# Four sixteen-head attention stages: the exponential of a step split by head and bank

## Chip, cores and metric

The kernel runs on one core of a Trainium2 chip. The metric is device time in microseconds (us) of one execution; lower is better. The core has TensorE (PE), VectorE (DVE), ScalarE (ACT), GpSimd (POOL) and SyncE (SP, which only starts DMAs). Each takes its own instructions in order, and semaphores order them among engines.

## The reference, cut to what matters

The network is a chain of 16 residual layers on X of shape 8 x 512 x 128. Four of them are attentions with 16 heads of 8 channels: `l0b` (no mask), and `l2a`, `l2b`, `l3a` (causal). What such a layer computes for each batch and head is, in short:

```
q, k, v = heads(x @ Wq), heads(x @ Wk), heads(x @ Wv)   # 16 heads of 8 channels
scores  = einsum('bhqd,bhkd->bhqk', q, k)               # 512 x 512, * 1/sqrt(8) and causal in l2a, l2b, l3a
attn    = softmax(scores, axis=-1)
out     = einsum('bhqk,bhkd->bhqd', attn, v)            # l2a, l2b, l3a: then a projection
```

The other twelve layers (experts, quantised feed-forward, other attentions) are not touched.

## The kernel before

All four attentions are built by `heads_attention_stage` (L475). Its work is cut into steps T. A step takes one pair of heads (hh = 0, 1) and one chunk c of the key tiles. A group of four heads (index g, four per batch) has L steps (index l): L = 8 in l0b, where a chunk is one tile of 128 keys against all 512 queries, and L = 6 in the causal stages, where the chunks are key tile 0 (512 query columns), key tile 1 (384) and key tiles 2 and 3 together (256 + 128 columns). With 8 batches, l0b has 256 steps and each causal stage 192.

Every engine walks the same loop over T, written out by hand:

- **TensorE**, step T: `scoresT(T)` (L707) makes the transposed scores of the step in `ps_t`, which has two PSUM banks, one per head. The two matmuls of a key tile, one per head, use different halves of the array's rows and run side by side. On even T follow `scores` (L733) for the steps T+3L and T+3L+1, the untransposed scores from which the maxima of the softmax are taken, in two buffers `ps_s`. On odd T follows `values` (L756), the product of the exponentials of the steps T-3 and T-2 with v. Then come the odd jobs of `spare` (L783), which share the one bank `ps_x`: projections q, k, v (g = 0, 1), the transposes "max", "back" (l = 3 in every group), "attnT", and the output projection.
- **ScalarE**, step T: at l = 2 first `read_group` (L839), a copy of the finished group's values (`oT`); then `exponentials(T)` (L830), one operation over both heads' banks, 1024 columns or 768, from `ps_t` to the SBUF tile `E`.
- **VectorE**, step T: `maxima` (L988) of step T+3L, the divisions, the splitting of the maxima, and in l0b the copies `l0b_y` (L1057).
- **GpSimd**, causal stages: `keep` (L905) zeroes the masked part of the exponentials.

`ps_t` is one buffer. So `scoresT(T)` waits until the exponential of step T-1 has ended, and the exponential of T waits for the matmuls of T; the wait of TensorE stands at the head of its queue, with `scores` or `values` of the step behind it. Only in the last steps (T from LAST = ALL - 3L + 2), when `scores` are all done, the two buffers `ps_s` join, and the transposed scores go round three buffers.

Of the kernel before, what the change touches and what calls it, by code (L numbers as in the profile page):

```python
# [474 lines left out]
def heads_attention_stage(core, name, w, wo=None, bo=None, qk_bias=None, v_bias=None, rope=None, eps=0.0,  # L475
# [10 lines left out]
    L = 2 * NC  # L486
# [9 lines left out]
    with ExitStack() as ctx:  # L496
# [147 lines left out]
        def _(sp):  # L644
# [11 lines left out]
            def place_stack(n, half):  # L656

                for a in range(2):
                    sp.wait_ge(pieces_stored[a].sem, pieces_stored[a].after(PLACES * (n + 1)))
                if n >= 2:  # L660
                    sp.wait_ge(scoresT_ready.sem, scoresT_ready.upto((n - 2) * STEPS + (2 * half + 2) * L))
                for a, dst in enumerate((qs[n % 2], ks[n % 2])):
                    for hh in range(2):
                        sp.dma_start(dst[64 * hh:64 * hh + STACK, 4 * half:4 * half + 4, :],
                                     stack[a, :, 2 * hh + half].rearrange("k d c s -> k d (c s)")).then_inc(stack_ready[half].sem, 16)
# [42 lines left out]
        def _(pe):  # L708
            def scoresT(T, b, g, l):
# [3 lines left out]
                if T <= LAST:  # L713
                    pe.wait_ge(probs_ready.sem, probs_ready.upto(T))
                elif T <= LAST + 2:
                    pe.wait_ge(scores_read.sem, scores_read.upto(ALL))
                else:
                    pe.wait_ge(probs_ready.sem, probs_ready.upto(T - 2))
                if l == 0 and g % 2 == 0:
                    pe.wait_ge(max_placed[g // 2].sem, max_placed[g // 2].after(2 * (b + 1)))  # L720
                    if b == 0 and g == 0:
                        pe.wait_ge(ones_placed.sem, ones_placed.after(4))
                off = 0
                for kt in k_chunks[c]:
                    n = S - first_q[kt]
                    for hh in range(2):
                        r = slice(64 * hh, 64 * hh + M_ROW + 3)
                        mm = pe.matmul(scores_room(T)[:, hh, off:off + n], ks[b % 2][r, j, kt * P:(kt + 1) * P],  # L728
                                       qs[b % 2][r, j, first_q[kt]:S], start=True, stop=True)
                    off += n  # L730
                mm.then_inc(scoresT_ready.sem, 1)
# [24 lines left out]
            def values(n):  # L756
# [3 lines left out]
                pe.wait_ge(probs_ready.sem, probs_ready.upto(2 * n + 2))  # L760
# [68 lines left out]
        def _(act):  # L829
            def exponentials(T, b, g, l):  # L830
                c, p = l // 2, l % 2
                n = T // 2
                act.wait_ge(scoresT_ready.sem, scoresT_ready.upto(T + 1))
                if n >= 3:
                    act.wait_ge(pv_ready.sem, pv_ready.upto(n - 2))
                act.activation(probs(n % 3, c, 0)[:, 2 * p:2 * p + 2, :], scores_room(T)[:, :, 0:width[c]],  # L836
                               ACT.Exp, scale=scale).then_inc(probs_ready.sem, 1)
# [60 lines left out]
        def _(pool):  # L898
# [6 lines left out]
            def keep(T, b, g, l):  # L905

                c, p = l // 2, l % 2
                pool.wait_ge(probs_ready.sem, probs_ready.upto(T + 1))
# [231 lines left out]
    scores_ready.per = scores_read.per = scoresT_ready.per = probs_ready.per = ALL  # L1140
# [2589 lines left out]
```

## Time and profile before

| | us |
|---|---|
| median of 3 runs | 3916.51 |
| the runs | 3915.03, 3926.91, 3916.51 |
| the profiled execution | 3924.91 |
| its span, first to last instruction | 3923.1 |
| steps of l0b in it, 528.9 to 945.3 | 416.4 |
| steps of l2a, 1956.8 to 2280.0 | 323.2 |
| steps of l2b, 2503.8 to 2830.5 | 326.7 |
| steps of l3a, 3066.9 to 3388.2 | 321.3 |

Over the whole span the page gives TensorE busy 72%, VectorE 67%, ScalarE 45%, GpSimd 44%. The program is a chain of 16 layers, so these shares say little for one layer; the stretches in the lower half of the table are read one by one. A row of a timeline gives the start, the duration, the engine and line, and in brackets how long the engine stood idle before and what ended it. PE is the matmul, PEld the weight load ahead of it; the wait of a matmul sits on its weight load, and since matmuls are pipelined, a matmul's row ends after the array is already free for the next. An operation of ScalarE can start before the row of the one before it ends.

### The profile page before, as it was taken

How to read it: one execution, taken by the hardware profiler on the slowest of the kernel's cores; microseconds unless marked ns; L12 is line 12 of the kernel's file. 1: busy time of each engine (PE TensorE's matmuls, PEld its weight loads, DVE VectorE, ACT ScalarE, POOL GpSimd, SP SyncE). 2: the span in 40 equal slices, each digit the busy share in tenths (PEclk: the TensorE clock that was granted, in tenths of full speed). 3: DMA queues.
4: the chain of work that ended last, by engine and by line, in shares of the span. 5: the costliest groups of instructions: out<-in, count | busy, mean ns of one | idle time of the engine just before them, and what ended most of it. 6: DMA issues, size and time to landing. Idle time of an engine off the chain costs nothing. (4 is left out here: it accounts for less than half of the span.)

```text
span 3923.1 us, 64375 instructions
## 1 busy us (share of the span) xinstructions
PE 2817.3 (72%) x22261; PEld 1768.3 (45%) x22261; DVE 2638.8 (67%) x5824; ACT 1783.6 (45%) x3184; POOL 1713.8 (44%) x2364
## 2 busy tenths in 40 slices
PE   6869267775693769569488856688656888677946
PEld 4769212221693449459233335233344333354535
DVE  5645478886455944344588858688677788595768
ACT  2423247665221324334256643566643466544633
POOL 7655422220546022232456443355543555445743
PEclk9979679998797759879699977799977899886977
DMA  6123232210231012002222100222000222000000
GB/s 191 45 72 103 56 96 78 87 61 30 79 93 45 0 64 70 16 23 70 71 75 75 59 1 2 90 74 75 26 0 24 84 82 76 2 1 1 1 3 19
DMA packets 220979, 208.00 MB, mean 53 GB/s; under 512 B 49671, under 2 KB 197831, under 8 KB 219896
## 3 DMA queue, kind: packets, MB, share of 16 engines
q1 hardware_dynamic: 208376, 178.69, 14.1%
q0 software_dynamic: 12288, 25.19, 2.1%
q8 instruction: 188, 3.08, 0.3%
q14 instruction: 127, 1.04, 0.1%
HBM read 103.94 MB, written 97.91 MB: 51 GB/s over the span
## 5 line engine op out<-in xcount | busy, mean ns | idle before, releaser
L993 DVE TENSOR_REDUCE l0b_negm<-l0b_ps_s 128x2 f32<-128x1024 f32 x256 | 304.1, 1219 | 51.5 <-PE l0b_ps_s L746 50.5
L836 ACT ACTIVATE l0b_E<-l0b_ps_t 128x1024 f32<-128x1024 f32 x242 | 247.8, 1024 | 117.6 <-PE l0b_ps_t L728 117.4
L993 DVE TENSOR_REDUCE l2b_negm<-l2b_ps_s 128x2 f32<-128x256 f32 (+3 forms) x256 | 196.3, 818 | 28.7 <-PE l2b_ps_s L751 28.6
L836 ACT ACTIVATE l2a_E<-l2a_ps_t 128x768 f32<-128x768 f32 (+1 forms) x182 | 160.4, 881 | 119.7 <-PE l2a_ps_t L728 118.9
L836 ACT ACTIVATE l3a_E<-l3a_ps_t 128x768 f32<-128x768 f32 (+1 forms) x182 | 160.4, 881 | 117.1 <-PE l3a_ps_t L728 116.3
L993 DVE TENSOR_REDUCE l3a_negm<-l3a_ps_s 128x2 f32<-128x256 f32 (+3 forms) x256 | 196.3, 818 | 16.6 <-PE l3a_ps_s L751 16.5
L993 DVE TENSOR_REDUCE l2a_negm<-l2a_ps_s 128x2 f32<-128x256 f32 (+3 forms) x256 | 195.9, 816 | 14.9 <-PE l2a_ps_s L751 14.8
L836 ACT ACTIVATE l2b_E<-l2b_ps_t 128x768 f32<-128x768 f32 (+1 forms) x182 | 160.3, 881 | 100.3 <-PE l2b_ps_t L728 99.5
L913 POOL TENSOR_SCALAR_AFFINE_SELECT l2b_E<-l2b_E 128x256 f32<-128x256 f32 x256 | 100.6, 409 | 175.9 <-ACT l2b_E L836 175.7
L913 POOL TENSOR_SCALAR_AFFINE_SELECT l2a_E<-l2a_E 128x256 f32<-128x256 f32 x256 | 101.3, 408 | 161.3 <-ACT l2a_E L836 159.2
L913 POOL TENSOR_SCALAR_AFFINE_SELECT l3a_E<-l3a_E 128x256 f32<-128x256 f32 x256 | 101.3, 409 | 159.7 <-ACT l3a_E L836 157.9
L728 PE MATMUL l0b_ps_t<-room_up,room_down 51*128 51x512 bf16 x484 | 96.2, 394 | 70.2 <-ACT l0b_E L836 60.9
L775 PE MATMUL l0b_ps_v<-l0b_E,l0b_v 128*32 128x512 f32 x1024 | 140.6, 621 | 3.7 <-ACT l0b_E L836 2.1
L2934 ACT ACTIVATE l0fb_hT<-l0fb_ps_u 128x512 f32<-128x512 f32 x85 | 50.8, 598 | 145.8 <-PE l0fb_ps_u L2872 144.3
L2934 ACT ACTIVATE l0fa_hT<-l0fa_ps_u 128x512 f32<-128x512 f32 x85 | 50.8, 598 | 144.7 <-PE l0fa_ps_u L2872 143.6
L728 PEld LDWEIGHTS l0b_ps_t<-room_up,room_down 51*128 51x128 bf16 x484 | 23.3, 93 | 204.5 <-ACT l0b_E L836 193.8
L746 PE MATMUL l0b_ps_s<-room_down,room_up 48*128 48x512 bf16 x512 | 87.8, 404 | 25.7 <-DVE l0b_negm L993 22.7
L2872 PE MATMUL l0fb_ps_u<-l0fb_xT,l0fb_own_up 128*128 128x128 f32 x680 | 94.3, 284 | 10.1 <-DVE l0fb_xT L3120 4.6
L2872 PE MATMUL l0fa_ps_u<-l0fa_xT,l0fa_own_up 128*128 128x128 f32 x680 | 94.1, 283 | 9.3 <-DVE l0fa_xT L3120 4.8
L775 PE MATMUL l2b_ps_v<-l2b_E,l2b_v 128*32 128x512 f32 (+3 forms) x1024 | 93.9, 463 | 8.9 <-POOL l2b_E L913 6.9
L775 PE MATMUL l2a_ps_v<-l2a_E,l2a_v 128*32 128x512 f32 (+3 forms) x1024 | 91.7, 453 | 4.9 <-ACT l2a_oT L844 2.3
L775 PE MATMUL l3a_ps_v<-l3a_E,l3a_v 128*32 128x512 f32 (+3 forms) x1024 | 91.6, 452 | 4.7 <-ACT l3a_oT L844 2.9
(982 smaller groups left out, 8703.0 us busy)
## 6 DMA issues: line engine op xcount, KB each, us to landing
room_up<-l0b_stack SPq DMA_DIRECT2D x32, 192.0 KB
room_down<-l0b_stack SPq DMA_DIRECT2D x32, 192.0 KB
room_up<-l2a_stack SPq DMA_DIRECT2D x32, 192.0 KB
room_down<-l2a_stack SPq DMA_DIRECT2D x32, 192.0 KB
room_up<-l2b_stack SPq DMA_DIRECT2D x32, 192.0 KB
room_down<-l2b_stack SPq DMA_DIRECT2D x32, 192.0 KB
room_up<-l3a_stack SPq DMA_DIRECT2D x32, 192.0 KB
room_down<-l3a_stack SPq DMA_DIRECT2D x32, 192.0 KB
```

The lines of the kernel that those rows point to most:

```text
L728: mm = pe.matmul(scores_room(T)[:, hh, off:off + n], ks[b % 2][r, j, kt * P:(kt + 1) * P], qs[b % 2][r, j, first_q[kt]:S], start=True, sto ...
L746: mm = pe.matmul(ps[:, hh, off:off + keys[qt]], qs[b % 2][r, j, qt * P:(qt + 1) * P], ks[b % 2][r, j, 0:keys[qt]], start=True, stop=not ca ...
L775: mm = pe.matmul(ps_v[32 * a:32 * a + 32, first_q[kt]:S], v_row[b % 2][:, kt, col:col + 32], e[:, a, off:off + w_k], start=(kt == 0), stop ...
L836: act.activation(probs(n % 3, c, 0)[:, 2 * p:2 * p + 2, :], scores_room(T)[:, :, 0:width[c]], ACT.Exp, scale=scale).then_inc(probs_ready.s ...
L913: kept = pool.affine_select(out=here, in_=here, compare_op=ALU.is_ge, fill=0.0, base=0, pattern=[[0, 2], [1, P]], channel_multiplier=-1)
L993: e = dve.tensor_reduce(negm[:, qt, :, j], ps_s[n % 2][:, :, off:off + keys[qt]], AX.X, ALU.max, negate=True)
L2872: mm = pe.matmul(ps_u[j % 4][:, c, :], own_up[j % 3][:, c * P:(c + 1) * P], xT[G % 2][:, k, :], start=True, stop=True)
L2934: a = act.activation(hT[j % 3][:, :, :], ps_u[j % 4][:, :, :], ACT.Gelu)
```

## The change

Each step's exponential becomes two operations, one per head and bank, each half as long in columns (512, or 384). Each of the two waits for its own head's matmul and adds one to `probs_ready`; a step thus counts two. `scoresT` adds one to `scoresT_ready` at the last matmul of each head, and the first matmul of head hh waits for the exponential of head hh of the step before. The other waits on the two semaphores have their counts doubled, so they wait for both heads as before.

```diff
@@ scoresT @@
-                if T <= LAST:
-                    pe.wait_ge(probs_ready.sem, probs_ready.upto(T))
-                elif T <= LAST + 2:
+                if LAST < T <= LAST + 2:
                     pe.wait_ge(scores_read.sem, scores_read.upto(ALL))
-                else:
-                    pe.wait_ge(probs_ready.sem, probs_ready.upto(T - 2))
...
+                before = T if T <= LAST else T - 2
                 off = 0
                 for kt in k_chunks[c]:
                     n = S - first_q[kt]
                     for hh in range(2):
+                        if kt == k_chunks[c][0] and before > 0 and not LAST < T <= LAST + 2:
+                            pe.wait_ge(probs_ready.sem, probs_ready.upto(2 * before - 1 + hh))
                         r = slice(64 * hh, 64 * hh + M_ROW + 3)
                         mm = pe.matmul(scores_room(T)[:, hh, off:off + n], ks[b % 2][r, j, kt * P:(kt + 1) * P],
                                        qs[b % 2][r, j, first_q[kt]:S], start=True, stop=True)
+                        if kt == k_chunks[c][-1]:
+                            mm.then_inc(scoresT_ready.sem, 1)
                     off += n
-                mm.then_inc(scoresT_ready.sem, 1)
@@ exponentials @@
-                act.wait_ge(scoresT_ready.sem, scoresT_ready.upto(T + 1))
                 if n >= 3:
                     act.wait_ge(pv_ready.sem, pv_ready.upto(n - 2))
-                act.activation(probs(n % 3, c, 0)[:, 2 * p:2 * p + 2, :], scores_room(T)[:, :, 0:width[c]],
-                               ACT.Exp, scale=scale).then_inc(probs_ready.sem, 1)
+                for hh in range(2):
+                    act.wait_ge(scoresT_ready.sem, scoresT_ready.upto(2 * T + 1 + hh))
+                    act.activation(probs(n % 3, c, 0)[:, 2 * p + hh, :], scores_room(T)[:, hh, 0:width[c]],
+                                   ACT.Exp, scale=scale).then_inc(probs_ready.sem, 1)
@@ place_stack, values, keep, end of the stage: the counts doubled @@
-                pe.wait_ge(probs_ready.sem, probs_ready.upto(2 * n + 2))
+                pe.wait_ge(probs_ready.sem, probs_ready.upto(2 * (2 * n + 2)))
...
-                pool.wait_ge(probs_ready.sem, probs_ready.upto(T + 1))
+                pool.wait_ge(probs_ready.sem, probs_ready.upto(2 * (T + 1)))
```

The order of the other work stays. On ScalarE in l0b, around the copy `oT` at l = 2 of a group, there stood before (each row one operation, or several with the same waits):

```order
L836 ACTIVATE l0b_E<-l0b_ps_t 128x1024 [waits pv_ready,scoresT_ready] x8
L844 ACTIVATE l0b_oT<-l0b_ps_v 128x512 [waits spare_ready,pv_ready]
L836 ACTIVATE l0b_E<-l0b_ps_t 128x1024 [waits pv_ready,scoresT_ready]
L883 ACTIVATE l0b_mT<-l0b_ps_x 24x512 [waits max_placed1,spare_ready]
L836 ACTIVATE l0b_E<-l0b_ps_t 128x1024 [waits pv_ready,scoresT_ready] x6
```

and with the change, a pair of rows for each step:

```order
L837 ACTIVATE l0b_E<-l0b_ps_t 128x512 [waits scoresT_ready,pv_ready]
L837 ACTIVATE l0b_E<-l0b_ps_t 128x512 [waits scoresT_ready]
L845 ACTIVATE l0b_oT<-l0b_ps_v 128x512 [waits spare_ready,pv_ready]
L837 ACTIVATE l0b_E<-l0b_ps_t 128x512 [waits scoresT_ready,pv_ready]
L837 ACTIVATE l0b_E<-l0b_ps_t 128x512 [waits scoresT_ready]
L884 ACTIVATE l0b_mT<-l0b_ps_x 24x512 [waits max_placed1,spare_ready]
```

The copy `oT` (l = 2) and the odd copies still stand between the exponentials of two steps, ahead of both heads.

On TensorE in l2a, around the third chunk (256 + 128 columns, l = 4 and 5), there stands with the change:

```order
L727 MATMUL l2a_ps_t<-room_up,room_down 128x384 [waits probs_ready] x2
L775 MATMUL l2a_ps_v<-l2a_E,l2a_v_1 32x512 [waits pv_read,probs_kept,probs_ready]
L775 MATMUL l2a_ps_v<-l2a_E,l2a_v_1 32x512 x3
L801 MATMUL l2a_ps_x<-identf,l2a_oT 128x128 [waits pv_read,spare_read]
L801 MATMUL l2a_ps_x<-identf,l2a_oT 128x128 x3
L727 MATMUL l2a_ps_t<-room_up,room_down 128x256 [waits probs_ready] x2
L727 MATMUL l2a_ps_t<-room_up,room_down 128x128 x2
L746 MATMUL l2a_ps_s<-room_down,room_up 128x256 [waits scores_read]
```

where before the pairs of `l2a_ps_t` read like this, one wait for both heads:

```order
L728 MATMUL l2a_ps_t<-room_up,room_down 128x384 [waits probs_ready]
L728 MATMUL l2a_ps_t<-room_up,room_down 128x384
L775 MATMUL l2a_ps_v<-l2a_E,l2a_v_1 32x512 [waits pv_read,probs_kept,probs_ready]
L775 MATMUL l2a_ps_v<-l2a_E,l2a_v_1 32x512 x3
L801 MATMUL l2a_ps_x<-identf,l2a_oT 128x128 [waits pv_read,spare_read]
L801 MATMUL l2a_ps_x<-identf,l2a_oT 128x128 x3
```

Now both matmuls of the first key tile wait, each for its own head, and the 128-column matmul of head 0 stands behind the one of head 1 that waits.

## Rows read from the trace of the kernel before

**Rows 1.** Stretches: us; PE, PEld, DVE, ACT, POOL busy; PEclk; DMA share; GB/s.
```profile
528.90:945.30 416.40, 327.66 (x2260) 88.10 (x2260) 339.48 (x483) 291.89 (x321) 92.55 (x179) 0.97 0.21 65
1956.80:2280.00 323.20, 269.19 (x2819) 118.32 (x2814) 254.44 (x500) 201.59 (x269) 176.44 (x339) 0.97 0.18 66
```

**Rows 2.** Groups of instructions, forms apart, 528 to 944 us.
```profile
L993 DVE TENSOR_REDUCE l0b_negm<-l0b_ps_s 128x2 f32<-128x1024 f32 x234 | 279.1, 1220 | 37.3 <-PE l0b_ps_s L746 36.3
L836 ACT ACTIVATE l0b_E<-l0b_ps_t 128x1024 f32<-128x1024 f32 x241 | 246.8, 1024 | 117.6 <-PE l0b_ps_t L728 117.4
```

**Rows 3.** The same view, 1956 to 2279 us.
```profile
L836 ACT ACTIVATE l2a_E<-l2a_ps_t 128x768 f32<-128x768 f32 x121 | 98.1, 811 | 84.3 <-PE l2a_ps_t L728 84.1
```

**Rows 4.** Waits, 528 to 944 us (last columns: us in total, times, longest).
```profile
PEld l0b_ps_t L728 <- ACT l0b_E L836: 193.8, 185, 1.7
...
DVE l0b_negm L993 <- PE l0b_ps_s L746: 36.3, 50, 3.1
```

**Rows 5.** Waits, 1956 to 2279 us.
```profile
DVE l2a_negm L993 <- PE l2a_ps_s L751: 13.4, 25, 0.9
```

**Rows 6.** Timeline of l0b (start us, us, engine, line, operation, [idle before]).
```profile
669.58 0.39 PE L728 MATMUL l0b_ps_t<-room_up,room_down 51*128 51x512 bf16 x2 [0.69 <-ACT l0b_E L836]
...
670.01 1.02 ACT L836 ACTIVATE l0b_E<-l0b_ps_t 128x1024 f32<-128x1024 f32 x1 [0.49 <-PE l0b_ps_t L728]
...
671.03 0.60 ACT L844 ACTIVATE l0b_oT<-l0b_ps_v 128x512 f32<-128x512 f32 x1
...
671.53 1.02 ACT L836 ACTIVATE l0b_E<-l0b_ps_t 128x1024 f32<-128x1024 f32 x1
...
671.61 0.10 PEld L746 LDWEIGHTS l0b_ps_s<-room_down,room_up 48*128 48x128 bf16 x2 [0.41 <-DVE l0b_negm L993]
...
672.60 0.39 PE L728 MATMUL l0b_ps_t<-room_up,room_down 51*128 51x512 bf16 x2 [0.60 <-ACT l0b_E L836]
...
673.92 0.66 PE L801 MATMUL l0b_ps_x<-identf,l0b_oT 128*128 128x128 f32 x4
...
674.51 0.39 PE L728 MATMUL l0b_ps_t<-room_up,room_down 51*128 51x512 bf16 x2
...
676.02 0.39 PE L728 MATMUL l0b_ps_t<-room_up,room_down 51*128 51x512 bf16 x2 [0.69 <-ACT l0b_E L836]
```

**Rows 7.** Timeline of l2a, one group and the end of the one before.
```profile
2157.04 0.34 PE L728 MATMUL l2a_ps_t<-room_up,room_down 51*128 51x256 bf16 x4 [0.33 <-ACT l2a_E L836]
...
2157.42 0.81 ACT L836 ACTIVATE l2a_E<-l2a_ps_t 128x768 f32<-128x768 f32 x1 [0.44 <-PE l2a_ps_t L728]
...
2158.29 0.39 PE L728 MATMUL l2a_ps_t<-room_up,room_down 51*128 51x512 bf16 x2
...
2159.80 0.39 PE L728 MATMUL l2a_ps_t<-room_up,room_down 51*128 51x512 bf16 x2 [0.57 <-ACT l2a_E L836]
...
2161.15 0.59 ACT L844 ACTIVATE l2a_oT<-l2a_ps_v 128x512 f32<-128x512 f32 x1
...
2161.69 0.81 ACT L836 ACTIVATE l2a_E<-l2a_ps_t 128x768 f32<-128x768 f32 x1
...
2162.55 0.34 PE L728 MATMUL l2a_ps_t<-room_up,room_down 51*128 51x384 bf16 x2
...
2164.41 0.34 PE L728 MATMUL l2a_ps_t<-room_up,room_down 51*128 51x256 bf16 x4
```

**Rows 8.** Timeline of TensorE in l2a: what can follow the values of 384 columns.
```profile
2216.12 0.34 PE L728 MATMUL l2a_ps_t<-room_up,room_down 51*128 51x256 bf16 x4 [0.34 <-ACT l2a_E L836]
...
2217.17 0.65 PE L804 MATMUL l2a_ps_x<-identf,l2a_ao 128*128 128x128 f32 x4
```

**Rows 9.** Timeline of ScalarE in the last steps of l0b.
```profile
937.72 1.07 ACT L836 ACTIVATE l0b_E<-l0b_ps_t 128x1024 f32<-128x1024 f32 x1
938.62 0.65 ACT L844 ACTIVATE l0b_oT<-l0b_ps_v 128x512 f32<-128x512 f32 x1
939.10 2.01 ACT L836 ACTIVATE l0b_E<-l0b_ps_s 128x1024 f32<-128x1024 f32 x2
```

More of the change, by code:

```diff
@@ L660, in place_stack @@
                 if n >= 2:
-                    sp.wait_ge(scoresT_ready.sem, scoresT_ready.upto((n - 2) * STEPS + (2 * half + 2) * L))
+                    sp.wait_ge(scoresT_ready.sem, scoresT_ready.upto(2 * ((n - 2) * STEPS + (2 * half + 2) * L)))
                 for a, dst in enumerate((qs[n % 2], ks[n % 2])):
@@ L1139, in heads_attention_stage @@
     spare_ready.per = spare_read.per = len(use)
-    scores_ready.per = scores_read.per = scoresT_ready.per = probs_ready.per = ALL
+    scores_ready.per = scores_read.per = ALL
+    scoresT_ready.per = probs_ready.per = 2 * ALL
     probs_kept.per = ALL * causal
```

## Prediction

> **What bounds the kernel now.** The page's shares mix 16 layers, so I read the four stages by stretch first, then the groups of instructions and the waits, and last the timeline of a few steps. By stretch no engine of l0b is full: VectorE 339 of 416 us, TensorE 328, ScalarE 292; in l2a TensorE has 269 of 323 and VectorE 254 [rows 1]. The waits say who holds whom. In l0b TensorE's weight loads stand 193.8 us for the exponential, 185 times [rows 4]; ScalarE stands 117 us for TensorE between 241 exponentials, 0.49 us each time [rows 2]. That is a loop: the matmuls of a step need the buffer that the exponential frees, and the exponential needs the matmuls. The timeline gives its parts [rows 6]: matmuls at 669.58, exponential at 670.01 (0.43 later), 1.02 long, and the next matmuls 0.06 after an exponential's end. A step is 0.43 + 1.02 + 0.06 = 1.51 us, as between 674.51 and 676.02. Other work sets the pace where it is longer than the loop: from 672.60, an odd step with `values` and the transposes "back", the next matmuls come 1.91 us later [rows 6]. In l2a the loop is 1.51 us for steps of 1024 columns, 1.25 for those of 768 (2157.04 to 2158.29), and step l = 3 with "back" takes 1.86 (2162.55 to 2164.41) [rows 7].
>
> **Prices of the new pieces.** A 512-column operation: the copy `oT`, 0.60 us [rows 6]. For 384 columns: 1024 columns take 1.024 us [rows 2] and 768 take 0.811 [rows 3], so 0.83 ns a column, and 384 come to 0.49. Two operations that are both ready overlap: the exponential at 937.72 is followed 0.90 later by the copy, and the copy (512 columns) 0.48 later by the next exponential [rows 9]. So the second half starts 0.48 after the first (0.37 for 384 columns, with the same 0.12 of overlap), and a step's two halves hold ScalarE 0.48 + 0.60 = 1.08 from first start to last end where one operation took 1.02. The split costs 0.06 us wherever the end of both is waited for.
> The Trainium skill ("ScalarE: Activation LUTs", What ACT_TABLE_LOAD costs) has an operation at 186 ns + 0.833 ns a column and an overlap of 93 ns. That would be 0.61 long, the second 0.52 after the first, so 0.11 dearer per step instead of 0.06. The trace's pitch of 0.48 is lower and I go by it; by the page the sum below, 9 us faster, would be about 10 slower, since 0.05 more a step is 0.05 / 0.12 of the 46 us that the second rival works out.
>
> **What the change removes and adds in l0b.** Take the pair of an even step T and an odd T+1, T's matmuls at 0, both heads ready because `values` before them took longer. First half at 0.43, second at 0.91, ends at 1.03 and 1.51. Head 0's matmul of T+1 goes at 1.09; the `scores` before it are out by then. Head 1's cannot go before 1.57. It stands at the head of TensorE's queue, and `values` is behind it. From there TensorE's own work sets the pace: 1.32 us until something can follow `values` (672.60 to 673.92) [rows 6]. The pair takes 1.57 + 1.32 = 2.89 where it took 3.02: 0.13 gained, although head 0 was handed over 0.48 us early. Its loop alone would be 1.09 a step; the gain is lost because `values` waits for the later head. Now the eight steps of a group:
> - l = 4, 5 and l = 6, 7: 0.13 each, 0.26 gained.
> - l = 0, 1 and the copy `oT` at l = 2: the copy needs the values of step 1, 1.45 us after that step's matmuls (669.58 to 671.03), and the next exponential follows 0.48 later, at 1.93. Before, it came at 1.95 (671.53) [rows 6]. Step 1's second matmul is 0.06 later than before. Nothing gained, 0.04 lost.
> - l = 2, 3: step 3's second matmul another 0.06 later, and then TensorE's 1.91 as before. 0.06 lost.
> A group gains 0.16. Of 32 groups three lie in the last steps, and eight (g = 2) don't gain, because VectorE is behind there: it has two maxima of 1.22 us and two copies per pair, and TensorE already waits for it at 671.61 [rows 6]. 21 groups make 3.4 us. Projections make the even steps of g = 0 and 1 longer than the loop, which moves these figures by little. In the last 22 steps (three buffers, operations 0.90 apart [rows 9]) a step costs 2 x 0.48 = 0.96: 1.2 lost. l0b: **2 us gained**.
>
> **The causal stages**, six steps a group, on rows of l2a [rows 7]:
> - l = 0, 1 with `oT`: the copy starts 1.35 after step 1's matmuls (2159.80 to 2161.15), the next exponential 0.48 later: 1.57 + 1.83 = 3.40. Before: 1.51 + 1.89 (2161.69) = 3.40. Nothing.
> - l = 2: 0.38 (the start of a 768-column exponential after its matmuls, 2157.04 to 2157.42) + 0.37 + 0.49 + 0.06 = 1.30 instead of 1.25. Step 3 is TensorE's 1.86 as before. 0.05 lost.
> - l = 4: 1.30 again, not earlier for head 0 either: in the four-matmul steps its last matmul stands behind head 1's wait. Step 5: TensorE could go on 1.05 after its matmuls (2216.12 to 2217.17 [rows 8]) and waited until 1.25. So 2.35 instead of 2.50: 0.15 gained.
> A group gains 0.10. That holds for 16 groups of a stage (g = 2, 3, and g = 0 of the last two batches; three in the last steps left out): 1.6. At g = 1 seven groups have the v projection in step 4, so only the gain of step 5 counts, 0.15: 1.1. Six times g = 0 is all projections and gains nothing. The last 16 steps lose 0.5. That makes 2.2 us a stage, **6.6 us** for three.
>
> **Edits at nothing.** GpSimd's `keep` and TensorE's `values` still wait for both heads; the halves end 0.06 later, and `values` reads exponentials two and three steps old. The doubled counts order nothing new. SP's wait in `place_stack` is for a step long done. The 832 more operations of ScalarE need room: they hold it some 0.06 us more a step, in l0b 292 + 16 of 414 us [rows 1]. No DMA is moved.
>
> **Sum.** 2.2 + 6.6, about 9 us of the profiled execution's 3924.9, whose span is 3923.1. That execution is 8.4 above the median 3916.5, and I take the same 9 from the median: **3907.5 us**. A measurement of this kernel tells 0.3% from no change, 11.7 us; the forecast lies just inside.
>
> **The rivals.**
> *Absorbed.* The small gains of TensorE meet VectorE (339 of 416 us in l0b [rows 1]) or are paid back by the four-matmul steps, where the change doesn't do what it says: 64 of 192 steps of each causal stage have no early handover. For: 0.1 us a group is little beside one late VectorE operation. Against: TensorE is the one waited for in l2a. Without the gain of steps 4 and 5 the time is 3910 to 3920. Chance 0.18.
> *Slower: the halves don't overlap.* What overlaps in rows 9 were operations that had long been ready. If the second half, with its own wait, starts only when the first has ended, every step that the loop sets costs 0.12 more: 0.48 a group on 21 groups of l0b, 0.36 or 0.24 on 23 of each causal stage, 10 + 3 x 7.5; and in the last steps 0.24 and 0.2 a step, 5 + 3 x 3. That is 46 more, 37 slower than before: 3954. It decides from 0.02 us a step (no gain left) and is visible from 0.054. Chance 0.20. The figures of the Trainium skill's page "ScalarE: Activation LUTs" lie between the two, at 3927.
> *Much faster.* Where `oT` holds ScalarE, TensorE no longer waits for it and gets to the next `scores` 0.1 to 0.3 us sooner. VectorE waits 36.3 us for them in l0b and 13.4 in l2a [rows 4, 5]. If half of such waits go and what hangs on them follows, 18 + 3 x 7 = 39 with the sum's 9 partly in it: 3872 to 3885. Against: VectorE's lead is two buffers, and it waits mostly where the loop is slow, which stays. Chance 0.20.
>
> **How the numbers follow.** The forecast has 0.42, from 3897 to 3915, as the 0.13 and 0.15 stand on differences of rounded rows. Of it 0.17 is faster by over 0.3% and 0.25 within. Absorbed: 0.15 within, 0.03 slower. No overlap: 0.17 slower, 0.03 within. Much faster: 0.18 faster, 0.02 within. Sum: faster 0.35, within 0.3% 0.45, slower 0.20. The range 3885 to 3932 leaves out the far half of the second and of the third rival.
>
> **What the next profile would show.** Halves of 0.60 us (512) and 0.49 (384); the second starting 0.48 and 0.37 after the first. In l0b the pairs l = 4, 5 take 2.89 us and the odd step 1.32; the exponential after `oT` is as late as before; the stretch of l0b is 414 us, those of the causal stages about 321, 324.5 and 319. A second half starting 0.60 after the first proves the slower rival; stages shorter by over 8 us, with VectorE's wait for `scores` well under 36 us, the faster one. Wrong would also be a head 0 loop near 1.09 us a step, which would say that `values` doesn't hold it.

## The result, and the profile after

The change made the kernel a little slower. The median is **3922.28 us** (3918.58 to 3926.67, 12 runs) against 3915.76 us before on the same chip (3908.68 to 3926.91, 12 runs). The ratio is 1.0017, with a 95% interval of 1.0009 to 1.0025: under the 0.3% that counts as a difference here, but on the other side of 1 than the 3907.5 us forecast. The range, 3885 to 3932, holds it.

The profiled execution took 3924.3 us with a span of 3922.6, the one of before 3924.9 with 3923.1, so these two single traces would say that nothing happened. This study therefore has four traces of the kernel before and two of the changed one, and the table of stage lengths below uses them all.

Stretches of the changed kernel: l0b, l2a, l2b, l3a, and behind them l3fa, a stage that the change doesn't touch. The columns are those of [rows 1].

```profile
529.40:942.90 413.50, 357.62 (x2262) 94.98 (x2260) 336.42 (x482) 305.04 (x576) 92.89 (x179) 0.98 0.21 65
1953.60:2276.50 322.90, 287.53 (x2818) 126.55 (x2814) 255.34 (x500) 211.93 (x461) 176.99 (x340) 0.97 0.18 66
2499.90:2829.90 330.00, 287.93 (x2796) 126.16 (x2791) 250.79 (x541) 220.37 (x480) 173.62 (x329) 0.94 0.18 64
3066.30:3386.20 319.90, 286.46 (x2819) 126.43 (x2814) 252.10 (x469) 211.44 (x461) 176.70 (x339) 0.98 0.19 66
3398.60:3550.70 152.10, 101.97 (x448) 75.88 (x448) 123.15 (x207) 60.74 (x133) 61.69 (x64) 0.77 0.00 1
```

The same stretches in the third trace of the kernel before (run e10_before_third, 3910.46 us, the nearest of the four to the median beside it):

```profile
530.80:941.10 410.30, 320.39 (x2254) 86.31 (x2254) 337.01 (x483) 291.60 (x321) 92.48 (x179) 0.99 0.22 66
1949.80:2271.50 321.70, 267.61 (x2818) 117.91 (x2814) 254.28 (x500) 201.44 (x269) 176.06 (x339) 0.97 0.18 66
2493.00:2822.90 329.90, 264.52 (x2794) 116.69 (x2790) 250.28 (x541) 210.74 (x288) 173.94 (x330) 0.94 0.18 64
3056.00:3377.10 321.10, 267.51 (x2818) 117.86 (x2814) 252.15 (x469) 201.40 (x269) 176.01 (x339) 0.97 0.18 66
3389.90:3540.30 150.40, 98.68 (x448) 74.32 (x448) 123.20 (x208) 60.58 (x133) 61.65 (x64) 0.78 0.00 1
```

The work is the same except on ScalarE (291.6 to 305.0 us in l0b: two overlapping halves take longer than one operation) and in TensorE's busy time (320 to 358 us): the matmuls of the two heads no longer lie side by side in every step. The stages, from the first exponential's start to the last one's end, in us:

| kernel | l0b | l2a | l2b | l3a | l3fa |
|---|---|---|---|---|---|
| before, 4 traces | 416.2, 413.2, 410.2, 411.0 | 323.1, 322.8, 321.6, 322.9 | 326.7, 330.1, 329.9, 330.0 | 321.1 to 321.2 | 150.4 in each |
| changed, 2 traces | 413.5, 412.5 | 322.9, 325.7 | 329.9, 336.5 | 319.9, 319.8 | 152.2 in both |
| expected | 414 | 321 | 324.5 | 319 | unchanged |

The groups and waits of the changed kernel, l0b except for the second line, which is of l2a:

```profile
L837 ACT ACTIVATE l0b_E<-l0b_ps_t 128x512 f32<-128x512 f32 x484 | 263.1, 598 | 93.9 <-PE l0b_ps_t L727 89.8
L837 ACT ACTIVATE l2a_E<-l2a_ps_t 128x384 f32<-128x384 f32 x244 | 106.7, 492 | 82.2 <-PE l2a_ps_t L727 81.6
```

```profile
PEld l0b_ps_t L727 <- ACT l0b_E L837: 168.5, 274, 1.7
...
DVE l0b_negm L994 <- PE l0b_ps_s L746: 35.4, 48, 3.5
```

The halves take 0.598 and 0.492 us, as priced. TensorE stands for the exponential 168.5 us instead of 193.8 [rows 4], but now 274 times instead of 185. VectorE's wait for `scores` is still there, 35.4 against 36.3 us. The pair of steps l = 4, 5 of one group, first TensorE, then ScalarE, whose row holds four halves:

```profile
739.22 0.39 PE L727 MATMUL l0b_ps_t<-room_up,room_down 51*128 51x512 bf16 x2
...
740.36 0.87 PE L727 MATMUL l0b_ps_t<-room_up,room_down 51*128 51x512 bf16 x2 [0.31 <-ACT l0b_E L837]
...
742.16 0.39 PE L727 MATMUL l0b_ps_t<-room_up,room_down 51*128 51x512 bf16 x2
...
739.71 2.22 ACT L837 ACTIVATE l0b_E<-l0b_ps_t 128x512 f32<-128x512 f32 x4 [1.02 <-PE l0b_ps_t L727]
```

The pair takes 742.16 - 739.22 = 2.94 us, where 2.89 was expected and 3.02 was before. The exponential starts 0.49 after its matmuls, not 0.43. The cause shows in ScalarE's instructions with their semaphores, as the trace holds them, here for the even step of that pair (start us, ns, what it is, and the count it waits for: `scoresT` that of the transposed scores, `pv` that of the `values` of an earlier pair of steps):

```
739.645   17  wait alone           scoresT
739.706  597  exponential, head 0 pv
740.201  591  exponential, head 1 scoresT
```

The exponential of head 0 has two waits and carries one of them, the one that the source writes first; the other becomes an instruction of its own ahead of it. The kernel before writes the wait for `scoresT` first, and its trace has that wait in the operation and the one for `pv`, long fulfilled, in the separate instruction. The change writes the wait for `pv` first, ahead of the loop over the heads, and the trace has it the other way round: the event that comes last now ends the separate wait, and the operation starts 0.061 us behind it.

The change swaps a second pair of waits in the same way, on TensorE. At l = 0 of the groups g = 0 and 2 the first matmul has a wait for the exponential and one for the placed maxima (`max_placed`). The kernel before writes the one for the exponential first; the changed one writes it inside the loop over the heads, behind the other. The trace has it as a separate instruction there, and the matmul carries the wait for `max_placed`, long fulfilled. What this costs shows in e6 below.

### The profile page after: what moved, and what is told of

Same layout as the page of the kernel before. It is cut to its first block and busy times, and to the rows that moved or that the text cites. A ratio compares the mean times of both kernels' runs of the same rounds, so it can differ in the third digit from the quotient of the medians.

```text
span 3922.6 us, 65207 instructions
## 1 busy us (share of the span) xinstructions
PE 2908.3 (74%) x22261; PEld 1800.6 (46%) x22261; DVE 2636.5 (67%) x5824; ACT 1827.5 (47%) x4016; POOL 1717.6 (44%) x2364
## 3 DMA queue, kind: packets, MB, share of 16 engines
q8 instruction: 188, 3.08, 0.3%
## 5 line engine op out<-in xcount | busy, mean ns | idle before, releaser
L837 ACT ACTIVATE l0b_E<-l0b_ps_t 128x512 f32<-128x512 f32 x484 | 263.1, 598 | 93.9 <-PE l0b_ps_t L727 89.8
L837 ACT ACTIVATE l2a_E<-l2a_ps_t 128x384 f32<-128x384 f32 (+1 forms) x364 | 172.0, 527 | 107.5 <-PE l2a_ps_t L727 106.3
L837 ACT ACTIVATE l3a_E<-l3a_ps_t 128x384 f32<-128x384 f32 (+1 forms) x364 | 171.9, 527 | 106.4 <-PE l3a_ps_t L727 105.4
L837 ACT ACTIVATE l2b_E<-l2b_ps_t 128x384 f32<-128x384 f32 (+1 forms) x364 | 172.7, 531 | 93.5 <-PE l2b_ps_t L727 92.4
L727 PE MATMUL l0b_ps_t<-room_up,room_down 51*128 51x512 bf16 x484 | 134.8, 392 | 33.8 <-ACT l0b_E L837 24.3
L727 PEld LDWEIGHTS l0b_ps_t<-room_up,room_down 51*128 51x128 bf16 x484 | 32.8, 93 | 190.6 <-ACT l0b_E L837 168.5
L727 PE MATMUL l2b_ps_t<-room_up,room_down 51*128 51x512 bf16 (+3 forms) x486 | 94.4, 316 | 13.2 <-ACT l2b_E L837 6.2
L727 PE MATMUL l3a_ps_t<-room_up,room_down 51*128 51x512 bf16 (+3 forms) x486 | 90.6, 307 | 10.0 <-ACT l3a_E L837 4.0
```

Source lines behind the costliest of these rows:

```text
L837: act.activation(probs(n % 3, c, 0)[:, 2 * p + hh, :], scores_room(T)[:, hh, 0:width[c]], ACT.Exp, scale=scale).then_inc(probs_ready.sem, 1)
```

## The experiments

The theory after the first trace: the split works as priced, and 0.06 us of its gain is lost in every step by the order of the two waits; what else is lost comes from collisions in the causal stages. The rivals: the early hand-over is worthless; or `values` behind head 1's wait is what must be moved.

**Wait order restored** (e1_wait_first), else as the change:

```diff
-                if n >= 3:
-                    act.wait_ge(pv_ready.sem, pv_ready.upto(n - 2))
                 for hh in range(2):
                     act.wait_ge(scoresT_ready.sem, scoresT_ready.upto(2 * T + 1 + hh))
+                    if hh == 0 and n >= 3:
+                        act.wait_ge(pv_ready.sem, pv_ready.upto(n - 2))
```

> The changed kernel with one thing moved: the exponential of head 0 states its wait for the matmul first and the wait for the values' buffer second, as the kernel before did. Theory W (wait order): in the changed kernel a separate semaphore row stands for the matmul's wait on ScalarE (677.80) and the exponential starts 0.06 later, 0.48 after a pair's matmuls where it was 0.43. Put back, it starts 0.43 after; the pair of steps in l0b falls from 2.94 to 2.89 us, and the whole by about 0.05 x 3 places a group on some 90 groups, 10 to 15 us, to 3907 to 3912. Rival H (hand-over): the loss comes from TensorE standing for head 1 and from VectorE, and the wait's order is hidden: 3920 to 3924, pairs at 2.94.

Measured: 3920.6 us against 3911.6 before, ratio 1.0025 (1.0015 to 1.0035). In l0b it does what was expected: 406.4 us.

```profile
734.45 0.39 PE L727 MATMUL l0b_ps_t<-room_up,room_down 51*128 51x512 bf16 x2
...
737.32 0.39 PE L727 MATMUL l0b_ps_t<-room_up,room_down 51*128 51x512 bf16 x2
...
734.87 2.16 ACT L837 ACTIVATE l0b_E<-l0b_ps_t 128x512 f32<-128x512 f32 x4 [0.96 <-PE l0b_ps_t L727]
```

The exponential starts 0.42 after the matmuls and the pair takes 2.87. But l2b took 335.0 us and l3a 324.7, and the time missed the 3907 to 3912 expected. So the order of the waits was a real cost in l0b, and the causal stages took as much back. What their rows show is this: in l2b four small conversions of VectorE take 1.20 us each, a collision described below, and the granted clock of l3a is 0.95, where the four traces of before and the two of the change have 0.97 and 0.98. Why it is lower there isn't known from this one trace.

**The other order in the kernel before** (e2_before_pv_first): there the two waits are swapped and nothing else.

```diff
-                act.wait_ge(scoresT_ready.sem, scoresT_ready.upto(T + 1))
                 if n >= 3:
                     act.wait_ge(pv_ready.sem, pv_ready.upto(n - 2))
+                act.wait_ge(scoresT_ready.sem, scoresT_ready.upto(T + 1))
```

> The kernel before, with only the order of the two waits ahead of the exponential swapped (the values' buffer first). Theory W: the exponential starts 0.48 after its matmuls instead of 0.43 in every step that the loop sets; with 185 waits of TensorE for it in l0b and about 117 in each causal stage that is up to 0.055 x 536 = 29 us slower, 3935 to 3945. Rival H: no change, 3914 to 3918.

Measured: 3949.72 us, ratio 1.0102 (1.0086 to 1.0117), above the 3935 to 3945 expected. The loop step of l0b is 1.57 us instead of 1.51, that of 768 columns 1.30 instead of 1.24, and l0b, l2a and l3a take 425.2, 335.0 and 331.3 us; l2b, at 326.7, is no longer than before. Two source lines in another order cost 38 us. Here the split's other effects are absent, so this is the cost of the order alone.

**The split in l0b alone, first try** (e3_l0b_only): the causal stages keep one operation, but raise both counts by two.

```diff
+                if not grouped:
+                    act.wait_ge(scoresT_ready.sem, scoresT_ready.upto(2 * T + 2))
...
+                                   ACT.Exp, scale=scale).then_inc(probs_ready.sem, 2)
+                    return
```

> The split of e1 in l0b alone; the causal stages issue one exponential and one wait a step as before. By my sum l0b gains 2 us and each causal stage 2.2, so this kernel stands at 3912 to 3915 and e1 6 us below it. If the causal stages are where the time is lost, this kernel is faster than e1. If both are the same as before, neither half of the change is worth anything once the wait is in its place.

Measured: 3923.73 us, ratio 1.0035 (1.0021 to 1.0048), where 3912 to 3915 was expected. This was no clean control. In its trace a causal exponential that raises its count by two carries no wait at all; both stand in a separate instruction, the loop steps are 1.56 and 1.29 us, and l2a and l3a took 327.3 and 326.1. l0b's steps were those of e1; its 412.2 us have a first batch of 61.0 where the other kernels with this order have 56.6 to 57.7.

**Heads whole** (e4_heads_whole): e1, and `scoresT` issues all key tiles of head 0 before those of head 1, so that the steps of four matmuls hand head 0 over early too.

```diff
-                for kt in k_chunks[c]:
-                    n = S - first_q[kt]
-                    for hh in range(2):
+                for hh in range(2):
+                    off = 0
+                    for kt in k_chunks[c]:
+                        n = S - first_q[kt]
```

> e1 with the transposed scores of a step issued head by head: in the steps of two key tiles (64 of 192 of a causal stage) both matmuls of head 0 go before the first of head 1, so head 0's exponential no longer waits for head 1's buffer. If that block counts, step 5's exponential of head 0 starts 0.4 us earlier and up to 0.1 us a group is gained, 1 to 3 us a stage, 3 to 8 us below e1. If TensorE's own work and the copy oT set the pace, it is the same as e1, or slower by up to 0.1 us a group where both heads are ready and their matmuls no longer run side by side.

Measured: 3912.01 us, ratio 1.0002 (0.9992 to 1.0012). l0b 407.0, l2a 319.5, l3a 318.3, each better than before; l2b 332.9, worse. Against e1 this is 8.6 us, of which l2a and l3a give 2.6 and 6.4. The part that this order of the matmuls gives shows in the steps: with the change and in e1 the matmul of head 1 at l = 0 of g = 0 goes 0.20 to 0.26 us behind that of head 0, with all other work of TensorE behind it; here both go at once, and the pair l = 0, 1 takes 4.10 instead of 4.29 us. That is 0.2 us a batch; the rest of l3a's 6.4 goes with its clock (0.97 here, 0.95 in e1), and one trace of each doesn't say whether the order caused that.

**Work between the heads** (e5_between): e4, and `scores` or `values` issued between the two heads' transposed scores.

```diff
                 if 0 <= T < ALL:
-                    scoresT(T, b, g, l)
+                    scoresT(T, b, g, l, 0)
...
+                if 0 <= T < ALL:
+                    scoresT(T, b, g, l, 1)
```

> As heads whole, and an even step's two scores, an odd step's values, are issued between the two heads' transposed scores, so that nothing stands behind head 1's wait but the next step. If my step in the prediction holds (the gain of the early hand-over is lost because values waits behind head 1), the pair of steps l = 4, 5 of l0b falls from the 2.88 us of heads whole to about 2.75 to 2.80, l0b from 407 to about 400, and the time to 3900 to 3908 if nothing is given back elsewhere. If the loops' gain is given back by collisions of VectorE and GpSimd and by TensorE's clock (theory C), the pair shortens all the same, but l2b stands at 330 to 340 and the time at 3908 to 3915. If the hand-over itself is worthless (theory H), the pair stays at 2.88 or more and the time at 3912 or above.

Measured: 3990.39 us, ratio 1.0195 (1.0178 to 1.0211). The pair in l0b, TensorE:

```profile
747.85 0.39 PE L727 MATMUL l0b_ps_t<-room_up,room_down 51*128 51x512 bf16 x1
...
748.93 0.39 PE L727 MATMUL l0b_ps_t<-room_up,room_down 51*128 51x512 bf16 x1 [0.25 <-ACT l0b_E L838]
749.25 1.07 PE L774 MATMUL l0b_ps_v<-l0b_E,l0b_v 128*32 128x512 f32 x8
750.25 0.39 PE L727 MATMUL l0b_ps_t<-room_up,room_down 51*128 51x512 bf16 x2
```

`values` is no longer behind head 1's wait, and it starts 0.32 after head 0's matmul. This pair, l = 4, 5, takes 750.25 - 747.85 = 2.40 us, less than the 2.75 to 2.80 expected. But it starts late, behind the transposes of l = 3, when ScalarE has caught up. The next pair, l = 6, 7, still takes 2.88, because head 1's matmul is now behind `values` (1.32 later) and ScalarE takes head 1 ahead of the next step's head 0. The pairs l = 0, 1 and l = 2, 3 of this group, g = 3, are longer than in e4 (3.52 and 3.63 against 3.08 and 3.47), and the group takes 12.42 us against 12.31. So early hand-over pays in a single pair, and this place gives nothing over a group. l0b took 426.2 us, and l2b 366.3 with a granted clock of 0.89. That `scores` waiting for VectorE hold up head 1 in the even steps fits the program's order, but isn't shown apart.

**The split in l0b alone, with increments of one** (e6_l0b_clean): e1 for l0b; the causal stages issue the operations that they issued before.

```diff
+                if not grouped:
+                    act.wait_ge(scoresT_ready.sem, scoresT_ready.upto(T + 1))
+                    if n >= 3:
+                        act.wait_ge(pv_ready.sem, pv_ready.upto(n - 2))
...
+                                   ACT.Exp, scale=scale).then_inc(probs_ready.sem, 1)
+                    return
```

> The split, with the wait order of the kernel before (transposed scores first), in l0b alone; the causal stages issue what they issued before, one operation and one increment a step. Theory C (each stage's gain is its own, the losses sit in l2b and l3a): l0b 406 to 408 instead of 416, the other three stages 322 to 323, 326 to 327, 321 as before, time 3902 to 3907. Theory H (the hand-over is worthless, only the draw of an execution differs): l0b within 2 us of 416 and the time within 3 us of the kernel before.

Measured: 3909.17 us (3898.32 to 3920.56), ratio 0.9991 (0.9977 to 1.0004). l0b 407.6, as theory C has it, the others 321.5, 326.1, 321.4. The time is above the 3902 to 3907 expected of theory C; the runs of this kernel spread over 22 us, and a gain over the kernel before isn't shown.

This control isn't wholly clean either: TensorE's two waits at l = 0 of g = 0 and 2 stay swapped. In l2a and l3a the matmul there starts 0.144 us after the exponential's end, where it starts 0.055 after it without a second wait and in the kernel before, and the pair l = 4, 5 ahead of it takes 2.58 us instead of 2.49. That is 0.09 us at 16 places of a stage at most. In the changed kernel and in e4 it is hidden: the step l = 5 takes 1.43 us with the swapped waits behind it and without. No run puts this pair of waits back.

**The bias later** (e7_bias_later): e4, and in l2b GpSimd's addition of the bias moved by four steps. This tests a collision seen in e4 and e1, and again in the second trace of the changed kernel, described below.

```diff
-                if g == 3 and l == 0 and out_normed and 0 <= b < B:
+                if g == 3 and l == 4 and out_normed and 0 <= b < B:
                     add_bias(b)
```

> Heads whole, with GpSimd's addition of the bias (1.27 us) moved in l2b from step l = 0 to step l = 4 of the last group of a batch. If VectorE's small maxima operation (0.2 to 0.3 us) stretches to 1.2 us because it falls on that addition, and TensorE's idle time and clock follow from it, l2b falls from 333 us to 325 to 328 and the time from 3912 to 3904 to 3908. If l2b lengthens for another reason (the pair of halves, TensorE's own order), it stays at 331 to 335 and the time at 3911 to 3914. If another VectorE operation meets the addition at its new place, l2b stays long with the stretched operation at l = 4.

Measured: 3908.33 us, ratio 0.9992 (0.9983 to 1.0001). l2b took 329.0 instead of 332.9 us, where 325 to 328 was expected, and the median lies 3.7 below that of e4 (another chip, where the kernel before has the same median to 0.01 us). VectorE's operation, first in e4, then here (mean ns of one behind the busy time):

```profile
L1006 DVE CAST l2b_m_piece<-l2b_m_tmp 128x32 bf16<-128x32 f32 x15 | 7.1, 476 | 0.5
```

```profile
L1006 DVE CAST l2b_m_piece<-l2b_m_tmp 128x32 bf16<-128x32 f32 x15 | 2.8, 187 | 0.5
```

The four stretched conversions (of 15) are gone, so the collision was worth about 3.7 us. 329.0 is still no better than before.

**The split everywhere but in l2b** (e9_not_l2b): e4, and l2b as before but for TensorE's swapped waits.

```diff
+    halves = not out_normed
...
+                if not halves:
+                    act.wait_ge(scoresT_ready.sem, scoresT_ready.upto(T + 1))
```

> The split of heads whole in l0b, l2a and l3a; l2b issues what the kernel before issues. If each stage keeps its own gain or loss (theory C), the stages are 407, 319.5, 326 to 330 and 318 us, and the time is 3903 to 3907, ahead of heads whole (3912.0 against 3911.6 before) by what l2b gave back there. If l2b's length swings by 3 to 4 us from execution to execution whatever is issued in it, the time is 3908 to 3912, no better than the bias moved (3908.3).

Measured: **3904.00 us** (3900.23 to 3906.73) against 3911.08 before, ratio **0.9980** (0.9971 to 0.9989). Time and stages lie where theory C had them. It beats both kernels: 7 us off the kernel before. Its stretches:

```profile
527.90:935.00 407.10, 356.01 (x2255) 94.55 (x2254) 335.49 (x483) 304.46 (x577) 92.85 (x179) 0.98 0.22 67
1944.70:2264.30 319.60, 285.50 (x2818) 123.99 (x2814) 255.40 (x500) 211.79 (x461) 176.83 (x339) 0.97 0.19 67
2488.10:2817.90 329.80, 263.67 (x2794) 116.81 (x2790) 250.45 (x541) 210.96 (x288) 174.49 (x330) 0.94 0.18 64
3051.10:3369.50 318.40, 284.58 (x2819) 123.70 (x2814) 253.28 (x469) 212.03 (x461) 176.74 (x339) 0.97 0.19 67
```

**More traces** (e8_before_again, e10_before_third, e12_before_fourth: the kernel before; e11_after_again: the changed one).

> The kernel before once more, for a second trace, since the first one came from an execution 8.4 us above the median. Stages of 416, 323, 327, 321 us again if they don't vary between executions, and then the gains and losses per stage can be read to 1 us; if l0b or another stage comes out shorter by some us, the differences of single traces tell only as much as that.

> The kernel before, a third trace. Its two traces came from executions 8 and 5 us above the medians beside them. If the stages outside the change draw one of two lengths (l3b 214.9 or 218.1, l3fa 150.2 or 152.2, l0a 171.5 or 173.5), this trace again shows each at one of the two values, and the four stages of the change at 411 to 416, 322 to 323, 326 to 330 and 321.

> The changed kernel, a second trace. If its time comes from its own stages, they stand at 413, 323, 330, 320 us again; if they were drawn, one or more differs by 3 us or more. The pair l = 4, 5 of l0b is 2.94 us in either case, as the wait order is fixed in the program.

> The kernel before, a fourth trace, with the same reading as the third: how far the length of each stage swings between executions of one program, and so which differences of single traces can be believed. Expected: pairs of steps to 0.01 us the same, whole stages within 1 us in l2a and l3a, within 5 us in l0b and l2b.

They took 3916.93, 3910.46, 3914.81 and, the changed kernel, 3931.65 us. The pairs of steps without projections (g = 2 and 3 of l0b, l2a and l3a) repeat to 0.01 us; whole stages don't. l3b, untouched, is 214.9 or 218.1 us long in either kernel; the first traces of both had 218.1. TensorE's granted clock goes with such differences. The last 30 us of l2b in the first and in the third trace of the kernel before, and the last 22 and 21 us of l3a's steps in that third trace and in the first of the changed kernel:

```profile
2800.00:2830.50 30.50, 21.85 (x244) 9.39 (x244) 12.28 (x44) 22.68 (x33) 15.89 (x33) 1.00 0.01 2
2792.40:2822.90 30.50, 22.78 (x208) 9.23 (x208) 9.83 (x41) 20.45 (x29) 16.64 (x31) 0.83 0.01 2
3354.70:3377.10 22.40, 16.77 (x152) 6.43 (x148) 2.45 (x8) 16.61 (x25) 10.15 (x23) 0.85 0.01 2
3365.30:3386.30 21.00, 14.52 (x152) 6.01 (x148) 2.42 (x8) 17.49 (x41) 10.39 (x23) 1.00 0.01 2
```

The first two are the same program, and its l2b took 326.7 and 329.9 us; at the lower clock the last 30.5 us hold 208 matmuls instead of 244. The last two hold the same matmuls. In the second trace of the changed kernel l2b took 336.5 us, and three of its batches show this (VectorE, then GpSimd, then TensorE):

```profile
2665.40 1.19 DVE L1007 CAST l2b_m_piece<-l2b_m_tmp 128x32 bf16<-128x32 f32 x1
2666.51 1.21 DVE L994 TENSOR_REDUCE l2b_negm<-l2b_ps_s 128x2 f32<-128x1024 f32 x1
...
2665.29 1.27 POOL L940 TENSOR_TENSOR XN<-XN,l2b_bo 128x512 f32<-128x512 f32 x1
...
2666.74 0.38 PE L796 MATMUL l2b_ps_x<-identb,l2b_m_piece 128*24 128x128 bf16 x4 [0.66 <-DVE l2b_m_piece L1007]
...
2670.10 0.50 PE L746 MATMUL l2b_ps_s<-room_down,room_up 48*128 48x384 bf16 x2 [1.92 <-DVE l2b_negm L994]
...
2670.96 1.93 PE L775 MATMUL l2b_ps_v<-l2b_E,l2b_v 128*32 128x512 f32 x8
```

The same place in the third trace of the kernel before:

```profile
2651.87 0.32 DVE L1006 CAST l2b_m_piece<-l2b_m_tmp 128x32 bf16<-128x32 f32 x1
2652.10 1.21 DVE L993 TENSOR_REDUCE l2b_negm<-l2b_ps_s 128x2 f32<-128x1024 f32 x1
...
2652.12 1.27 POOL L939 TENSOR_TENSOR XN<-XN,l2b_bo 128x512 f32<-128x512 f32 x1
```

In the kernel before, the small conversion starts 0.25 us before GpSimd's addition and takes 0.32. In the first trace of the changed kernel it starts 0.31 before (0.39 long). In the second it starts 0.11 after, and takes 1.19 us, to the end of the addition. VectorE's reduction beside the addition takes 1.21 in the kernel before, as always. TensorE waits 0.66 for the converted piece, then 0.39 and 1.92 for the reductions that come late; of these waits the first trace has only the last (1.85). Then the granted clock falls to 0.50, the lower of its two levels. It does so behind that wait in the first trace too, but from 2664.5 to 2667.9 there and from 2668.4 to 2675.2 here, so that here the matmuls ahead of `values` take 0.50 instead of 0.34 and `values` itself 1.93 for eight instead of 1.24. The Trainium skill ("SBUF — State Buffer", Who interferes with whom) has it that a conversion on VectorE in its two-port mode and a GpSimd operation exclude each other for a whole instruction; the trace agrees, with 1.19 us where the same conversion takes 0.19 with the addition moved away.

The collision is not new with the change. In l2a the kernel before already shows it, and so the trace that the prediction was made from:

```profile
L1006 DVE CAST l2a_m_piece<-l2a_m_rest 128x32 bf16<-128x32 f32 x15 | 7.9, 527 | 0.5
```

A mean of 527 ns says that some are far longer than the others: five of the 15 take 1.19 us, each beside an operation of GpSimd of 1.27 us (`q_turn`, L624). A subtraction beside them (`m_tmp`) takes 1.21. l3a has the same, and so have the other three traces. With the change these conversions are short, and six of the 15 subtractions take 1.21 instead of one. The change moved the collision from one operation to its neighbour in l2a and l3a, and in its second trace brought it into l2b, where the kernel before has none.

The clock's share can be read by itself. In l2a of the second trace of the changed kernel TensorE waits for VectorE equally long at the same place of two batches (times of one and of the other):

```profile
2054.42 0.34 PE L746 MATMUL l2a_ps_s<-room_down,room_up 48*128 48x384 bf16 x2 [1.52 <-DVE l2a_negm L994]
...
2057.15 0.66 PE L801 MATMUL l2a_ps_x<-identf,l2a_oT 128*128 128x128 f32 x4 [0.48 <-ACT l2a_mT L884]
...
2096.40 0.34 PE L746 MATMUL l2a_ps_s<-room_down,room_up 48*128 48x384 bf16 x2 [1.53 <-DVE l2a_negm L994]
...
2099.14 1.12 PE L801 MATMUL l2a_ps_x<-identf,l2a_oT 128*128 128x128 f32 x4 [0.28 <-ACT l2a_mT L884]
```

After an idle time of 1.52 us the clock stays up (1.00 from 2050 to 2092) and the transposes take 0.66; after 1.53 it falls (0.50 from 2098.3 to 2105.1) and they take 1.12. The batch is 44.6 us long instead of 42.0. l3fa shows the same on a larger scale: in both traces of the changed kernel it is 1.8 us longer than in all four of before, with the same instructions, TensorE busy 102.0 instead of 98.7 us and a clock of 0.77 instead of 0.78. It doesn't follow from the split as such: e1, e4, e7 and e9, which have it, are back at 150 us there.

## Why the prediction was wrong

The medians put the change 6.5 us above the kernel before, and the forecast had it 9 below, so 15 us are to be found. By its own steps:

- **Prices of the pieces: right.** 0.60 and 0.49 us, and the second half 0.494 after the first (expected 0.48) and 0.387 (0.37). Two operations overlap by 0.597 - 0.494 = 0.103. The Trainium skill ("ScalarE: Activation LUTs", What ACT_TABLE_LOAD costs) has 93 ns, and this case's trace lies between that and the 0.12 of the prediction. The rival "the halves don't overlap" is out, and so is "much faster": VectorE's wait for `scores` stayed.
- **"First half at 0.43": wrong, and this is the first step that failed.** The start of an exponential was taken from [rows 6] as if the diff left it alone. The change moved the `pv` wait ahead, and "Edits at nothing" doesn't list it, so it was priced at nothing without a reason. It cost 0.06 us at each exponential that the loop waits for. With the order restored the steps come out as worked out. The eight steps of group g = 3 of l0b, medians over the middle batches, start to start:

| steps | before | expected | changed | wait order restored (e4) |
|---|---|---|---|---|
| l = 0, 1 | 3.03 | 3.07 | 3.14 | 3.08 |
| l = 2, 3 | 3.42 | 3.48 | 3.53 | 3.47 |
| l = 4, 5 | 3.02 | 2.89 | 2.94 | 2.88 |
| l = 6, 7 | 3.02 | 2.89 | 2.94 | 2.88 |
| sum | 12.49 | 12.33 | 12.55 | 12.31 |

  Expected 0.16 gained, changed 0.06 lost, restored 0.18 gained. Restored, l0b takes 406.4 to 407.6 us in five of the six kernels that have it (e1, e4, e6, e7, e9; e3 is the sixth), 5 to 7 less than the 412.5 and 413.5 of the change. The clock doesn't make this difference: in the third trace of before, the second of the change and that of e1 it stays up within l0b once it has risen at its start (0.99 over the stage in each), and l0b takes 410.2, 412.5 and 406.4. So the order of two waits cost 6 us there, and with it restored the split gained 3.8, where 2 were expected. The groups g = 2, written off for VectorE's sake, gain too: 12.48 before, 12.31 restored. In the whole kernel the wait order isn't enough: e1, with it restored, is still 1.0025 over the kernel before.
- **"`values` waits for the later head, and the gain is lost": right as a description.** Head 0's matmul of the odd step comes 1.14 us after that of the even one (1.09 was worked out, 1.08 with the order restored), and the next even step 1.80 after that, so `values` does hold the loop. e5 has 0.48 us back in one pair of four and loses more in the others.
- **The last steps of l0b: right.** 1.2 us were to be lost; from the first exponential of the last batch to the end of the stage it is 40.6 us instead of 39.3 in three of the four traces of before (41.0 in the first), though this difference has the wait order in it too.
- **The causal stages, 2.2 us each: the second step that failed.** The pair l = 4, 5 is right: 2.41 instead of 2.49 us, where 2.35 instead of 2.50 was expected, and 2.35 is reached with the order restored. But the groups don't keep it. The four groups of a middle batch of l3a, medians, from the first matmul of a group to that of the next:

| group | before | expected | changed | heads whole (e4) |
|---|---|---|---|---|
| g = 0 | 11.84 | 11.84 | 12.10 | 11.84 |
| g = 1 | 12.23 | 12.08 | 12.23 | 12.10 |
| g = 2 | 8.93 | 8.83 | 8.85 | 8.74 |
| g = 3 | 8.61 | 8.51 | 8.55 | 8.76 |
| batch | 41.61 | 41.26 | 41.73 | 41.44 |

  The batch was to be 0.35 us shorter and is 0.12 longer. The largest error is the term "g = 0 is all projections and gains nothing": it lost 0.26, because head 1's matmul goes 0.26 behind head 0's there and TensorE's own work stands behind it. e4, which hands head 0 over early in the steps of four matmuls as well, has this back; the rival "absorbed" was right about those steps. So l3a's 1.3 us (319.9 and 319.8 against 321.2) are no proof of the mechanism. They lie in the last 22 us of its steps, where the clock fell before (0.85) and not with the change (1.00). That gain was not forecast, so here the number is luck. l2a did not gain (322.9 and 325.7 against 322.6 on average), though e4, e7 and e9 have 319.5 to 319.6 there.
- **l2b: not foreseen.** 324.5 us expected, 329.9 and 336.5 measured. The first has no stretched conversion and is as long as three of the four traces of before; the 326.7 that the expectation started from is the odd one. The second has three in a row, and its 6.6 us more lie in those batches and the one behind them. The prediction moved steps by tenths of a microsecond and did not ask what lies beside VectorE's small operations on GpSimd. That margin was 0.25 us.
- **The baseline.** The stage lengths of "What the next profile would show" were counted from one trace whose l0b took 416.2 us at a granted clock of 0.97; the other three have 410.2 to 413.2 at 0.98 and 0.99. The changed l0b hit the expected 414 and yet gained nothing.

The account against the mean of the four traces of before (l0b 412.7, l2a 322.6, l2b 329.2, l3a 321.2): +0.3, +1.7, +4.0 and -1.3, with 1.8 us in l3fa and 1.6 in l2fb, 8 us together. The spans of the two traces are 11 us above the mean of those four, because the second one (3931.65) is longer than any of the 12 runs of the first comparison; the medians differ by 6.5. So the account is one of these two traces, and part of it may be chance. What is shown is the cost of the wait order in l0b (6 us), the steps of the causal groups, and the price of the collision in l2b (about 3.7 us, in e7). Not settled are the clock's falls, whether l3fa and l2fb belong to the change at all, and why the split without the collision (e7) leaves l2b at 329 instead of below.

## What to carry to other kernels

When a diff reorders waits, look up for each instruction which wait is fulfilled last in the trace, and see that the operation itself carries this one: in l0b 0.06 us a step decided between gain and loss. Before adding up gains of 0.1 us, take several traces of the kernel as it is, and compare steps, not totals: pairs of steps repeat to 0.01 us while stages of one and the same kernel swing by 2 to 6 us. Add up whole groups, too: a pair that starts early has gained nothing if the next one is longer by as much. And look at the means of small operations: one of 527 ns among others of 180 is a collision. Apply such a split stage by stage and keep it only where the stage's own length falls; here that was three of four.

## What was not expected of the hardware

- The order of two waits ahead of one operation costs 0.06 us when the later event sits in the separate instruction: 38 us (1.0102) over the kernel before, in e2.
- An operation that raises its count by two, in e3, carries no wait: loop steps of 1.56 us instead of 1.51.
- On TensorE the same order costs 0.09 us: in e6 the matmul starts 0.144 us after the exponential's end instead of 0.055.
- A VectorE conversion of 32 columns takes 0.18 to 0.44 us, and 1.19 us when it starts 0.11 us after a GpSimd addition of 1.27; a reduction from PSUM beside the same addition isn't touched (1.21).
- At equal idle times, 1.52 and 1.53 us, TensorE's clock stayed at the upper level in one batch and fell in the other, at a price of 2.6 us for the batch.
